# Reordering the attention of layer 2 in a vision-transformer tower on one Trainium2 core: four key products, exponentials and turned probabilities in another order, one filler product

## The chip, the cores and the metric

The kernel runs on one core of a Trainium2 chip. The metric is the device time of one execution in microseconds; where several executions were timed, their median. A profile is one execution, taken by the hardware profiler; its times count from the first instruction. Five engines run their own instruction streams and wait for each other on semaphores: TensorE (PE, with its weight loads as PEld), VectorE (DVE), ScalarE (ACT), GpSimd (POOL) and SyncE (SP).

## The reference

32 images of 84x84 are cut into 5x5 patches, so N = 25 tokens each, T = 800 tokens, C = 192 channels. A patch embedding and four post-norm layers follow. The part of this case is the third of the four, called layer 2 in the kernel, with 12 heads of 16 channels and two sets of queries and keys:

```python
def _L1_attn_ref(x, Wq, Wk, Wv, lambda_p, Wo, bo):
    q = (x @ Wq).reshape(B, N, 2, H, D).transpose(2, 0, 3, 1, 4)
    k = (x @ Wk).reshape(B, N, 2, H, D).transpose(2, 0, 3, 1, 4)
    v = (x @ Wv).reshape(B, N, H, D).transpose(0, 2, 1, 3)
    out1 = _attn(q[0], k[0], v)
    out2 = _attn(q[1], k[1], v)
    out = out1 - jnp.exp(lambda_p) * out2
    return out.transpose(0, 2, 1, 3).reshape(B, N, C) @ Wo + bo
...
h = _layernorm(h + _L1_attn_ref(h, ...), axis=-1)
```

Before it stand a linear attention (layer 0) and a mixture of 8 experts, 2 per token (layer 1); behind it an attention whose queries, keys and values come through adapters (layer 3), which the kernel computes with the same helpers as its "call 1".

## The kernel before

The program is written engine by engine, and the order on each engine is the order of the text; nothing is scheduled by a tool. The stage of this case runs from about 170 to 220 us.

The images form G = 8 groups of 4 images (100 tokens). Queries and keys come from split products (`split_job`, L1035 to L1041: five products of 400 columns each) for two halves of the tokens, 400 each; the first half serves groups 0 to 3, the second groups 4 to 7. ScalarE copies a query stack to `qT` (`queries_done`, L1191) or a key stack to `k_bd` (`keys_done`, L1360). A key stack is written four times, each copy multiplied by the mask of one head of four (`HQ` = 4), so that one product makes the scores of four heads. For the second half the stack of job 0 goes another way: ScalarE copies it once to `hwT`, and GpSimd makes the masked copies (L651).

A group g passes through these steps, each on one engine:

- PE, `scores(g)` (L962): 24 products in two or more banks of PSUM. For g >= 2 it waits until VectorE has read the group two before.
- DVE, `shift(g)`: the maximum (L1836) and the difference to `s1` (L1837).
- ACT, `exp_out(g)` (L1368): exponentials to `e1`, which has two buffers (g % 2). In layer 2 it waits for `p1_ready` of group g - 2, since GpSimd reads that buffer in `add_sets`.
- DVE, `norm(g)`: sum (L1846), reciprocal (L1847), factor with lambda (L1850, 24 columns), and the scaled exponentials in place (L1851, 600 columns).
- POOL, `add_sets(g)` (L640, L641): the two sets added to `p1`.
- PE, `turn(g)` (L972): the probabilities turned into bank 4.
- ACT, `p1T_out(g)` (L1191): the copy of bank 4 to `p1T`.
- PE, `times_v(g)` (L985): 12 products with the block-diagonal values `v_bd` into bank 5. It waits for `p1T_out(g)` and for `o_out(g - 1)`.
- ACT, `o_out(g)` (two copies, L1191): bank 5 to `oa` and `ob`.
- PE, `project(t)` (L996, L997) of a tile of 128 tokens, once its groups are there.

GpSimd also places the values in `v_bd` (`place_values`, L631) between these steps. VectorE's order is written out: shift 0, shift 1, norm 0, shift 2, norm 1, shift 3, norm 2, norm 3, shift 4, shift 5, norm 4, shift 6, norm 5, shift 7, norm 6, norm 7. `keep_busy` (L684) issues products whose result nobody reads; it stands at several places where PE waits. Scores 4 wait for `qk_act` 10, which is ScalarE's last query copy of the second half (`split_out(1, 5)`), and for `qk_pool`, GpSimd's masked keys.

Of the kernel before, what the change touches and what calls it, by code (L numbers as in the profile page):

```python
# [20 lines left out]
ALU = mybir.AluOpType  # L21
# [18 lines left out]
HALF = T // 2  # L40
# [20 lines left out]
HQ = 4  # L61
# [19 lines left out]
def rows(t):  # L81
    return min(128, T - 128 * t)


def view(ap, dims):

    return bass.AP(tensor=ap.tensor, offset=ap.offset, ap=[list(ap.ap[0])] + [list(d) for d in dims])


def build(nc, io):  # L90
    with ExitStack() as ctx:
        def sb(name, shape, dt=F32, scope=ctx):
            return scope.enter_context(nc.sbuf_tensor(name, shape, dt))

        def sem(name):
            return ctx.enter_context(nc.semaphore(name))

        ps = ctx.enter_context(nc.psum_tensor("ps", [128, 8, 512], F32))


        consts = sb("consts", [128, sum(w for _, w in CONSTS)])
        w0a, w0b = (sb(n, [r, sum(w for _, w in cols)]) for n, r, cols in (("w0a", 128, W0A), ("w0b", CB + 1, W0B)))
        w1a, w1b = (sb(n, [r, sum(w for _, w in cols)]) for n, r, cols in (("w1a", 128, W1A), ("w1b", 104, W1B)))

        def col(pack, cols, name, r0=0, r1=None):

            at = 0
            for n, width in cols:
                if n == name:
                    return pack[r0:r1 if r1 else pack.shape[0], at:at + width]  # L110
                at += width
            raise KeyError(name)

        ident = col(consts, CONSTS, "ident")
        head_mask1 = col(consts, CONSTS, "mask1")
# [59 lines left out]
        hwT = sb("hwT", [128, 32 * B], scope=late)  # L175
# [59 lines left out]
        k_bd = sb("k_bd", [128, 3, HQ, T])  # L235
# [67 lines left out]
        qk_ready, qk_act, qk_dve, qk_pool = sem("qk_ready"), sem("qk_act"), sem("qk_dve"), sem("qk_pool")  # L303
        s1_ready, s1_shifted, s1_exp = sem("s1_ready"), sem("s1_shifted"), sem("s1_exp")
# [190 lines left out]
        def _(pool):  # L495
# [138 lines left out]
            def add_sets(g):  # L634

                pool.wait_ge(e_scaled, g + 1)
                if g >= 2:
                    pool.wait_ge(p1T_ready, g - 1)
                blk = e1[:, g % 2, :, :].rearrange("p (a b c) m -> p a b c m", a=2, b=3)
                pool.tensor_tensor(p1[:, g % 2, 0:2, :, 0:N], blk[:, :, 0], blk[:, :, 1], ALU.add)  # L640
                pool.tensor_tensor(p1[:, g % 2, 2, :, 0:N], blk[:, 0, 2], blk[:, 1, 2], ALU.add).then_inc(p1_ready, 1)  # L641
# [5 lines left out]
            low_parts(1)  # L647
            add_sets(0)
            pool.wait_ge(qk_act, 5)
            for h in (0, 2):  # L650
                pool.tensor_tensor(k_bd[:, 0, h:h + 2, HALF:2 * HALF], view(hwT[:, 0:1], [[0, 2], [1, HALF]]),  # L651
                                   view(head_mask1[:, h:h + 1], [[1, 2], [0, HALF]]), ALU.mult).then_inc(qk_pool, 1)
            add_sets(1)
            pool.wait_ge(p1_ready, 2)
            place_values(0, 1, 0, 4)
# [17 lines left out]
        def last_group(t):  # L673

            return (128 * t + rows(t) - 1) // GT
# [3 lines left out]
        def _(pe):  # L679
# [274 lines left out]
            def scores(call, g, slots):  # L954
                if g >= 2:
                    pe.wait_ge(s1_shifted, G * call + g - 1)
                for bank, slot, row, stack in slots:
                    for i in range(IG):
                        tok = GT * g + N * i
                        keys = k_bd[row:row + 64, stack, :, tok:tok + N]  # L960
                        at = tok - HALF * (g // 4)
                        mm = pe.matmul(ps[32 * i:32 * i + 32, 2 * (g % 2) + bank, 4 * N * slot:4 * N * slot + 4 * N],  # L962
                                       qT[row:row + 64, stack, g // 4, at:at + 32], keys, start=True, stop=True)
                mm.then_inc(s1_ready, 1)

            def turn(call, g):
                n = G * call + g
                pe.wait_ge(p1_ready, n + 1)
                if g >= 1:
                    pe.wait_ge(p1T_done, n)  # L970
                for b in range(3):
                    mm = pe.transpose(ps[:, 4, 128 * b:128 * b + 128], p1[:, g % 2, b, :, :], ident[:, :])  # L972
                mm.then_inc(p1T_ready, 1)

            def times_v(call, g):
                n = G * call + g
                pe.wait_ge(p1T_done, n + 1)
                if g % 4 == 0:
                    pe.wait_ge(v_placed, 32 * call + 16 * (g // 4) + 16)
                if g >= 1:  # L980
                    pe.wait_ge(o1_done, n)
                for b, i in ((0, 0), (1, 0), (2, 0), (0, 1), (1, 1), (2, 1), (0, 2), (1, 2), (2, 2), (0, 3), (1, 3), (2, 3)):
                    rr = 64 * (b % 2)
                    at = (128 if b == 2 else 0) + N * i
                    mm = pe.matmul(ps[rr:rr + 64, 5, at:at + N], v_bd[:, IG * g + i, b, :],  # L985
                                   p1T[:, g % 2, b, 32 * i:32 * i + N], start=True, stop=True)
                mm.then_inc(o1_ready, 1)

            def project(call, t, wa, wb):
                pe.wait_ge(o1_done, G * call + last_group(t) + 1)  # L990
                if t >= 4 and t % 2 == 0:

                    pe.wait_ge(summed, PAIRS * (1 + call) + t // 2 - 1)
                cols = slice(128 * t, 128 * t + rows(t))
                out = ps[0:rows(t), PROJ_BANKS[t // 2], (t % 2) * C:(t % 2) * C + C]
                pe.matmul(out, oa[:, cols], wa, start=True, stop=False)  # L996
                pe.matmul(out, ob[:, cols], wb, start=False, stop=True).then_inc(proj_ready, 1)  # L997
# [73 lines left out]
            split_job(1, 5)  # L1071
            times_v(0, 0)
            turn(0, 1)
            pe.wait_ge(qk_act, 10)
            pe.wait_ge(qk_pool, 2)
            scores(0, 4, slots1)
            scores(0, 5, slots1)
            times_v(0, 1)
# [7 lines left out]
            turn(0, 4)  # L1086
            project(0, 1, wo1a, wo1b)
            times_v(0, 4)
            project(0, 2, wo1a, wo1b)
            turn(0, 5)  # L1090
            times_v(0, 5)
            turn(0, 6)
            project(0, 3, wo1a, wo1b)
# [95 lines left out]
        def _(act):  # L1189
            def copy(out, in_):  # L1190
                return act.activation(out, in_, ACT.Copy)  # L1191
# [161 lines left out]
            def queries_done(stack, n, src):  # L1353

                copy(qT[:, stack, n, 0:HALF], src).then_inc(qk_act, 1)

            def keys_done(m, stack, n, src):

                for h in range(HQ):
                    ins = act.activation(k_bd[0:m, stack, h, n * HALF:n * HALF + HALF], src, ACT.Copy, scale=head_mask1[0:m, h:h + 1])  # L1360
                ins.then_inc(qk_act, 1)

            def exp_out(call, g):
                act.wait_ge(s1_shifted, G * call + g + 1)
                if call == 0 and g >= 2:
                    act.wait_ge(p1_ready, g - 1)
                k = 12 if call else 24
                act.activation(e1[:, g % 2, 0:k], s1[:, g % 2, 0:k], ACT.Exp, scale=D1 ** -0.5).then_inc(s1_exp, 1)  # L1368

            def p1T_out(call, g):  # L1370
                act.wait_ge(p1T_ready, G * call + g + 1)
                if g >= 2 or call:
                    act.wait_ge(o1_ready, G * call + g - 1)
                copy(p1T[:, g % 2, :, :], ps[:, 4, 0:384]).then_inc(p1T_done, 1)

            def o_out(call, g):
                act.wait_ge(o1_ready, G * call + g + 1)
                copy(oa[:, GT * g:GT * g + GT], ps[:, 5, 0:GT])
                copy(ob[0:CB, GT * g:GT * g + GT], ps[0:CB, 5, 128:128 + GT]).then_inc(o1_done, 1)
# [13 lines left out]
            def split_out(n, job):  # L1393

                kind, stack = QK_ORDER[job]
                act.wait_ge(qk_ready, 6 * n + job + 1)
                src = ps[:, QK_BANKS[n][job], 0:HALF]
                if kind == "q":
                    queries_done(stack, n, src)
                else:  # L1400
                    keys_done(128, stack, n, src)
# [11 lines left out]
            split_out(1, 2)  # L1413
            p1T_out(0, 0)
            exp_out(0, 2)
            split_out(1, 3)
            exp_out(0, 3)
            split_out(1, 4)
            split_out(1, 5)
            p1T_out(0, 1)  # L1420
            o_out(0, 0)
            o_out(0, 1)
            exp_out(0, 4)
            p1T_out(0, 2)
            exp_out(0, 5)
            o_out(0, 2)
            p1T_out(0, 3)
            exp_out(0, 6)
            o_out(0, 3)
            p1T_out(0, 4)  # L1430
# [591 lines left out]
```

## Time and profile before

| | |
|---|---|
| median of 3 runs | 288.29 us |
| the three runs | 285.99, 288.29, 294.93 us |
| the profiled execution | 286.87 us |
| its span, first to last instruction | 285.1 us |
| PE, DVE, ACT, POOL busy | 258.6, 162.9, 121.3, 123.6 us |

The profiled execution's time is 1.8 us longer than its span: what lies before the first and behind the last instruction. A busy share is an average over stages, and idle time of an engine matters only where another waits for it. In a row of the timeline stand start, duration, engine, line, operation, output and inputs, shapes, and how many instructions the row merges; brackets at the end give the idle time before it and what ended it. A product of PE in 32-bit floats leaves two records, so x24 are 12 products of the program.

### The profile page before, as it was taken

The page shows a single profiled execution, that of the slowest core. Times are in us where ns is not written, and L with a number is a line of the kernel's source. Part 1 is how long each engine was busy: PE and PEld are TensorE (multiplying, and loading weights), DVE is VectorE, ACT ScalarE, POOL GpSimd, SP SyncE. Part 2 cuts the span into 40 slices and gives each one's busy share as a digit, 9 for nine tenths or more (in the row PEclk, how much of TensorE's full clock was granted, in tenths as well). Part 3 has the DMA queues.
Part 4 walks back from the last instruction along what each step waited for, and adds up shares of the span by engine and source line. Part 5 has one row for each costly group of instructions (what it writes and reads, how often), then busy time and mean ns, then how long its engine had stood idle before and what let it go on. Part 6 is the DMA issues. An engine that isn't in the chain of part 4 may idle for free.

```text
span 285.1 us, 6559 instructions
## 1 busy us (share of the span) xinstructions
PE 258.6 (91%) x2545; PEld 218.3 (77%) x2545; DVE 162.9 (57%) x486; ACT 121.3 (43%) x347; POOL 123.6 (43%) x191
## 2 busy tenths in 40 slices
PE   8989998976999999999999978998899799999990
PEld 8968678644999999999999538887777657667780
DVE  4676886885321332212330099899896474475874
ACT  5567868312442334433244005776441203763420
POOL 8762210316456655777432326857623100254311
PEclk9997999999999999999999999999689999999996
DMA  7999960161298999999200330000000000000002
GB/s 242 385 426 420 273 274 2 40 226 41 59 366 284 330 317 335 361 322 318 112 16 28 103 100 0 2 2 2 2 5 2 0 1 0 2 2 0 2 14 75
DMA packets 10113, 39.15 MB, mean 137 GB/s; under 512 B 1594, under 2 KB 5434, under 8 KB 7291
## 3 DMA queue, kind: packets, MB, share of 16 engines
q1 hardware_dynamic: 8163, 34.81, 33.9%
q0 software_dynamic: 1920, 3.93, 4.9%
q8 instruction: 20, 0.33, 0.4%
q14 instruction: 10, 0.08, 0.1%
HBM read 35.54 MB, written 3.19 MB: 136 GB/s over the span
## 4 chain that ended last, share of the span: by engine, by line
PE 66%; DVE 19%; ACT 4%; POOL 3%; issue 3%; DMA 3%; SPq 0%; POOLq 0%; ACTq 0%; DVEq 0%
PE ps L925 14%; PE ps L903 10%; PE ps L913 5%; PE ps L985 5%; PE ps L951 4%; PE ps L1121 3%; PE ps L972 2%; PE ps L996 2%; PE ps L962 2%; DVE s L1837 2%; PE ps L710 2%; DVE st L1836 2%; PE ps L810 2%; PE ps L997 1%; DVE st L1846 1%
## 5 line engine op out<-in xcount | busy, mean ns | idle before, releaser
L631 POOL COPY v_bd<-v_f 32x192 f32<-32x192 f32 x64 | 23.0, 359 | 34.3 <-ACT v_f L1191 30.4
L1321 ACT ACTIVATE hid<-ps,w1t 128x128 f32<-128x128 f32 x72 | 19.9, 376 | 34.7 <-PE ps L914 31.1
L577 POOL DMA_INDIRECT y_rows<-ys,to_row x20 | 19.8, 990 | 25.6 <-DVE ys L1793 23.2
L571 POOL DMA_INDIRECT xs<-x_rows,from_row x20 | 19.7, 983 | 22.0 <-PE ps L891 10.5
L1775 DVE COPY xga<-ps 128x128 f32<-128x128 f32 x20 | 5.8, 291 | 40.2 <-PE ps L891 39.9
L547 POOL TENSOR_TENSOR rstd<-veps,neg_half 128x2 f32<-128x2 f32 (+1 forms) x16 | 10.6, 664 | 41.6 <-DVE veps L1645 41.5
L925 PE MATMUL ps<-w1t,hid 128*128 128x192 f32 x144 | 24.6, 326 | 0.0
L684 PE MATMUL ps<-w1a,consts 128*128 128x384 f32 x66 | 22.7, 492 | 1.3 <-DVE h_tok L1627 1.3
L925 PEld LDWEIGHTS ps<-w1t,hid 128*128 128x128 f32 x144 | 23.3, 190 | 0.0
L985 PEld LDWEIGHTS ps<-p1T,v_bd 128*64 128x64 f32 x384 | 17.0, 142 | 5.3 <-issue 3.1
L985 PE MATMUL ps<-p1T,v_bd 128*64 128x25 f32 x384 | 18.6, 225 | 1.9 <-ACT p1T L1191 1.7
L684 PEld LDWEIGHTS ps<-w1a,consts 128*128 128x128 f32 x66 | 12.1, 190 | 9.8 <-DVE h_tok L1627 2.2
L903 PE MATMUL ps<-xga,w1t 128*128 128x128 f32 x144 | 18.7, 280 | 0.5 <-DVE xga L1775 0.5
L903 PEld LDWEIGHTS ps<-xga,w1t 128*128 128x128 f32 x144 | 17.2, 191 | 1.4 <-issue 0.7
L1836 DVE TENSOR_REDUCE st<-ps 128x24 f32<-128x600 f32 (+2 forms) x24 | 11.1, 462 | 12.2 <-PE ps L962 12.2
L1368 ACT ACTIVATE e<-s 128x600 f32<-128x600 f32 (+1 forms) x16 | 9.4, 586 | 14.2 <-DVE s L1837 14.2
L1360 ACT ACTIVATE k_bd<-ps,consts 128x400 f32<-128x400 f32 (+1 forms) x24 | 12.3, 600 | 0.8 <-PE ps L1041 0.8
L962 PE MATMUL ps<-k_bd,qT 64*32 64x100 f32 x576 | 11.4, 271 | 0.9 <-ACT qT L1191 0.9
L1837 DVE TENSOR_TENSOR s<-ps,st 128x600 f32<-128x600 f32 (+2 forms) x24 | 11.3, 470 | 0.8
L962 PEld LDWEIGHTS ps<-k_bd,qT 64*32 64x32 f32 x576 | 8.0, 113 | 4.8 <-issue 2.7
L1777 DVE COPY xgb<-ps 64x128 f32<-64x128 f32 x40 | 11.1, 278 | 0.6
L1793 DVE TENSOR_TENSOR ys<-ps,w1t 128x192 f32<-128x192 f32 x12 | 4.3, 357 | 12.4 <-PE ps L925 12.4
(301 smaller groups left out, 667.0 us busy)
## 6 DMA issues: line engine op xcount, KB each, us to landing
w1t<-in_wt SPq DMA_DIRECT2D x12, 1256.0 KB, 11.0
w1t_mid<-in_wt SPq DMA_DIRECT2D x3, 1256.0 KB, 11.4
w1t_top<-in_wt SPq DMA_DIRECT2D x3, 1256.0 KB, 10.9
pat<-in_pat SPq DMA_DIRECT2D x6, 496.0 KB, 5.8
w1t_low<-in_wt SPq DMA_DIRECT2D x2, 1256.0 KB, 7.5
w1a<-in_w1a SPq DMA_DIRECT2D x1, 1322.0 KB
y<-y_rows SPq DMA_DIRECT2D x6, 192.0 KB, 3.4
w1b<-in_w1b SPq DMA_DIRECT2D x1, 835.2 KB
```

The source lines that it names most:

```text
L571: pool.indirect_dma_start(xs[:, b, :], None, io["x_rows"], bass.IndirectOffsetOnAxis(from_row[:, j:j + 1], 0)).then_inc(gathered[b], 16)
L577: pool.indirect_dma_start(io["y_rows"], bass.IndirectOffsetOnAxis(to_row[:, j:j + 1], 0), ys[:, b, :], None).then_inc(scattered[b], 16)
L631: pool.tensor_copy(dst, src).then_inc(v_placed, 1)
L684: pe.matmul(ps[:, bank, 0:width], ident, w1a[:, 0:width] if width > 128 else ident, start=True, stop=True)
L903: mm = pe.matmul(hidden_out(j, k), w[:, 128 * k:128 * k + 128], xga[:, j % 2, :], start=(opens and k % HALF_HC == 0), stop=not opens, skip ...
L913: pe.matmul(hidden_out(j, k), w[0:CB, tail], xgb[0:CB, j % 2, :], start=(opens and k == 0), stop=not opens, skip_group_check=True)
L925: mm = pe.matmul(ps[:, Y_BANK[j % 2], 0:C], hid[:, j % 2, 128 * k:128 * k + 128], w[:, OUT_AT + C * k:OUT_AT + C * k + C], start=(k == 0), ...
L962: mm = pe.matmul(ps[32 * i:32 * i + 32, 2 * (g % 2) + bank, 4 * N * slot:4 * N * slot + 4 * N], qT[row:row + 64, stack, g // 4, at:at + 32 ...
L985: mm = pe.matmul(ps[rr:rr + 64, 5, at:at + N], v_bd[:, IG * g + i, b, :], p1T[:, g % 2, b, 32 * i:32 * i + N], start=True, stop=True)
L1321: ins = act.activation(hid[:, j % 2, 128 * k:128 * k + 128], hidden_out(j, k), ACT.Relu, bias=weights(j)[:, B1_AT + k:B1_AT + k + 1])
L1836: link(dve.tensor_reduce(top2, src, AX.X, ALU.max))
L1837: ins = dve.tensor_tensor(s, src, over(top2, N), ALU.subtract)
```

## The change

Five edits, all in the attention of layer 2. No arithmetic changes, except that one product more is computed and not read.

1. GpSimd masks the key stack in four products of 400 columns, one per head, where it used two of 800 columns; PE waits for four.
2. PE gets one 384-column filler product into bank 2 ahead of scores 4, behind a wait for VectorE's shift of group 3.
3. PE turns group 5 ahead of projection 2.
4. ScalarE does the exponentials of group 3 ahead of the key copies of job 3 (`split_out(1, 3)`), where they stood behind them.
5. ScalarE copies the turned probabilities of group 2 ahead of the exponentials of group 4, and those of group 3 ahead of `o_out` of group 2.

```diff
@@ GpSimd
             pool.wait_ge(qk_act, 5)
-            for h in (0, 2):
-                pool.tensor_tensor(k_bd[:, 0, h:h + 2, HALF:2 * HALF], view(hwT[:, 0:1], [[0, 2], [1, HALF]]),
-                                   view(head_mask1[:, h:h + 1], [[1, 2], [0, HALF]]), ALU.mult).then_inc(qk_pool, 1)
+            for h in range(HQ):
+                pool.tensor_tensor(k_bd[:, 0, h, HALF:2 * HALF], hwT[:, 0:HALF],
+                                   view(head_mask1[:, h:h + 1], [[0, HALF]]), ALU.mult).then_inc(qk_pool, 1)
             add_sets(1)
@@ PE
             turn(0, 1)
+            pe.wait_ge(s1_shifted, 4)
+            keep_busy(2, 1, 384)
             pe.wait_ge(qk_act, 10)
-            pe.wait_ge(qk_pool, 2)
+            pe.wait_ge(qk_pool, HQ)
             scores(0, 4, slots1)
...
             times_v(0, 4)
+            turn(0, 5)
             project(0, 2, wo1a, wo1b)
-            turn(0, 5)
             times_v(0, 5)
@@ ScalarE
             exp_out(0, 2)
+            exp_out(0, 3)
             split_out(1, 3)
-            exp_out(0, 3)
             split_out(1, 4)
             split_out(1, 5)
             p1T_out(0, 1)
             o_out(0, 0)
             o_out(0, 1)
+            p1T_out(0, 2)
             exp_out(0, 4)
-            p1T_out(0, 2)
             exp_out(0, 5)
+            p1T_out(0, 3)
             o_out(0, 2)
-            p1T_out(0, 3)
             exp_out(0, 6)
```

ScalarE between the exponentials of group 2 and the copy p1T of group 1, before (`e1` is an exponential, `k_bd` a masked key copy, `qT` a query copy):

```order
L1368 ACTIVATE e1<-s1 128x600
L1360 ACTIVATE k_bd<-ps,consts 128x400 x4
L1368 ACTIVATE e1<-s1 128x600
L1191 ACTIVATE qT<-ps 128x400 x2
L1191 ACTIVATE p1T<-ps 128x384
```

and after (its lines are numbered two higher from here on):

```order
L1370 ACTIVATE e1<-s1 128x600 x2
L1362 ACTIVATE k_bd<-ps,consts 128x400 x4
L1193 ACTIVATE qT<-ps 128x400 x2
L1193 ACTIVATE p1T<-ps 128x384
```

One exponential has moved ahead of four key copies; what follows is the same.

ScalarE behind that, from the two `o_out` of groups 0 and 1, before (`p1T` is the copy of the turned probabilities, `oa` and `ob` are one `o_out`):

```order
L1191 ACTIVATE oa<-ps 128x100
L1191 ACTIVATE ob<-ps 64x100
L1368 ACTIVATE e1<-s1 128x600
L1191 ACTIVATE p1T<-ps 128x384
L1368 ACTIVATE e1<-s1 128x600
L1191 ACTIVATE oa<-ps 128x100
L1191 ACTIVATE ob<-ps 64x100
L1191 ACTIVATE p1T<-ps 128x384
L1368 ACTIVATE e1<-s1 128x600
```

and after:

```order
L1193 ACTIVATE oa<-ps 128x100
L1193 ACTIVATE ob<-ps 64x100
L1193 ACTIVATE p1T<-ps 128x384
L1370 ACTIVATE e1<-s1 128x600 x2
L1193 ACTIVATE p1T<-ps 128x384
L1193 ACTIVATE oa<-ps 128x100
L1193 ACTIVATE ob<-ps 64x100
```

The copy of group 2 now stands ahead of the exponentials of groups 4 and 5, that of group 3 behind both.

PE at scores 4 and at projection 2, as one difference (L684 is the filler, L962 scores 4 and 5, L972 a turn, L985 products with the values, L996 and L997 a projection):

```order
 L985 MATMUL ps<-p1T,v_bd 64x25 x12
 L972 MATMUL ps<-consts,p1 128x128 x3
+L684 MATMUL ps<-w1a,consts 128x384
 L962 MATMUL ps<-k_bd,qT 32x100 x48
 L985 MATMUL ps<-p1T,v_bd 64x25 x12
...
-L996 MATMUL ps<-w1a,oa 128x192
-L997 MATMUL ps<-w1b,ob 128x192
-L972 MATMUL ps<-consts,p1 128x128 x3
+L972 MATMUL ps<-consts,p1 128x128 x3
+L996 MATMUL ps<-w1a,oa 128x192
+L997 MATMUL ps<-w1b,ob 128x192
 L985 MATMUL ps<-p1T,v_bd 64x25 x12
```

The filler has come between the turn of group 1 and scores 4, and the turn of group 5 has moved ahead of a projection.

## Rows read from the trace of the kernel before

**Rows 1.** Page: busy time, share of the span and instructions of each engine.

```profile
PE 258.6 (91%) x2545; PEld 218.3 (77%) x2545; DVE 162.9 (57%) x486; ACT 121.3 (43%) x347; POOL 123.6 (43%) x191
```

**Rows 2.** Chain of waits, 188 to 203 us: start us, us, what.

```profile
187.68 0.70 DVE st L1836
...
195.12 0.11 DVE st L1850
...
200.42 0.48 ACT p1T L1191
200.91 0.04 issue
200.95 1.21 PE ps L985 x24
```

**Rows 3.** Timeline of DVE, 188 to 206 us.

```profile
190.24 1.50 DVE L1850 TENSOR_TENSOR st<-st,lam 128x24 f32<-128x24 f32 x1
191.77 0.78 DVE L1851 TENSOR_TENSOR e<-e,st 128x600 f32<-128x600 f32 x1
...
195.12 0.18 DVE L1850 TENSOR_TENSOR st<-st,lam 128x24 f32<-128x24 f32 x1
...
198.20 0.77 DVE L1836 TENSOR_REDUCE st<-ps 128x24 f32<-128x600 f32 x1
...
201.20 0.77 DVE L1846 TENSOR_REDUCE st<-e 128x24 f32<-128x600 f32 x1
...
204.28 0.78 DVE L1836 TENSOR_REDUCE st<-ps 128x24 f32<-128x600 f32 x1 [0.91 <-PE ps L962]
```

**Rows 4.** Timeline of POOL, 181 to 213 us.

```profile
183.32 0.96 POOL L617 TENSOR_TENSOR x_lo<-xpa,x_hi 128x400 fp32r<-128x400 f32 x1 [0.27 <-POOL v_bd L631]
...
188.69 3.01 POOL L651 TENSOR_TENSOR k_bd<-hwT,consts 128x800 f32<-128x800 f32 x2
192.64 0.62 POOL L640 TENSOR_TENSOR p<-e 128x200 f32<-128x200 f32 x1 [0.94 <-DVE e L1851]
193.21 0.41 POOL L641 TENSOR_TENSOR p<-e 128x100 f32<-128x100 f32 x1
...
212.15 0.40 POOL L641 TENSOR_TENSOR p<-e 128x100 f32<-128x100 f32 x1
```

**Rows 5.** Timeline of ACT, 189 to 203 us.

```profile
192.46 2.08 ACT L1360 ACTIVATE k_bd<-ps,consts 128x400 f32<-128x400 f32 x4
194.36 0.76 ACT L1368 ACTIVATE e<-s 128x600 f32<-128x600 f32 x1
194.96 0.96 ACT L1191 ACTIVATE qT<-ps 128x400 f32<-128x400 f32 x2
...
199.81 0.70 ACT L1368 ACTIVATE e<-s 128x600 f32<-128x600 f32 x1 [0.98 <-DVE s L1837]
200.42 0.47 ACT L1191 ACTIVATE p1T<-ps 128x384 f32<-128x384 f32 x1
```

**Rows 6.** Timelines of PE, 164 to 172, 189 to 206 and 204 to 220 us.

```profile
165.27 3.49 PE L684 MATMUL ps<-w1a,consts 128*128 128x384 f32 x10 [1.26 <-DVE h_tok L1627]
...
195.97 1.40 PE L962 MATMUL ps<-k_bd,qT 64*32 64x100 f32 x96 [0.92 <-ACT qT L1191]
197.30 1.11 PE L985 MATMUL ps<-p1T,v_bd 128*64 128x25 f32 x24
198.34 0.55 PE L972 MATMUL ps<-consts,p 128*128 128x128 f32 x3
...
200.95 1.21 PE L985 MATMUL ps<-p1T,v_bd 128*64 128x25 f32 x24 [1.15 <-ACT p1T L1191]
202.92 1.25 PE L962 MATMUL ps<-k_bd,qT 64*32 64x100 f32 x48
204.11 1.90 PE L985 MATMUL ps<-p1T,v_bd 128*64 128x25 f32 x24
...
212.89 0.55 PE L972 MATMUL ps<-consts,p 128*128 128x128 f32 x3
...
216.72 1.11 PE L985 MATMUL ps<-p1T,v_bd 128*64 128x25 f32 x24
```

**Rows 7.** Windows: us, busy us of each engine, granted clock, DMA share, GB/s.

```profile
198.30:201.70 3.40, 2.25 (x30) 1.69 (x29) 3.33 (x5) 1.85 (x5) 2.95 (x9) 1.00 0.00 0
201.70:208.50 6.80, 6.80 (x138) 5.79 (x136) 5.65 (x11) 2.62 (x8) 3.49 (x8) 0.51 0.01 2
```

## The prediction

> **What bounds the kernel now.** I read the page first, then the windows by stage, then the chain of waits, then the timeline of each engine where the chain runs. On the page PE is 91% busy and no other engine is over 57% [rows 1], which says little, because the diff touches 30 us of 285: the attention of layer 2, from 188 to 220 us. There the chain of waits leaves PE. From 187.7 to 195.2 us it runs on DVE alone, then over POOL and ACT's copy of the turned probabilities, and returns to PE at 200.95 [rows 2]. So DVE sets the pace from 188 to about 203: every one of its instructions starts as the last ends [rows 3]. PE only waits at two places: 0.92 us before scores 4 and 5, for ACT's last query copy, and 1.15 us before the products with the values of group 2, for ACT's copy p1T [rows 6]. After that the granted clock is half (0.51, the 1.2 GHz level) from 201.7 to 208.5 us [rows 7], and PE is full: products with the values take 1.90 us there and 1.11 elsewhere [rows 6]. From 212.9 PE runs almost without a gap to the end of the stage. What the change is worth is therefore read from three things: when scores 4 starts, when p1T of group 2 is copied, and whether the clock is halved.
>
> **The four products on POOL.** Before, two products of 128x800 take 1.53 us each and 3.01 together [rows 4]. While they run, DVE's tiny product L1850 (0.18 us at 195.12) takes 1.50 and ends when POOL's second product ends [rows 3, 4]. So the change's idea is right: DVE loses 1.3 us there. The price of a 128x400 product is not in the trace; its bounds are half of 1.53 (0.76) and 0.96, which another POOL product of 128x400 takes. The sums of 200 and 100 columns (0.62 and 0.41) leave 0.20 fixed per instruction, so I take (1.53 - 0.20) / 2 + 0.20 = 0.86, with starts 0.81 apart. Then POOL's second piece ends at 188.69 + 0.81 + 0.86 = 190.36; L1850, waiting since 190.24, gets in and ends 190.54; the third piece runs to 191.40; DVE's L1851 (0.78) to 192.18; the fourth piece to 193.04. DVE is 0.37 us ahead (192.18 against 192.55), not 1.3, since L1851 collides in its turn.
>
> What happens to POOL matters more. It still owes the sums of group 1 (L640, L641: 0.98 together [rows 4]), and they end at 193.04 - 0.05 + 0.96 = 193.95, against 193.62. They cannot come earlier: in either kernel POOL's 3.0 us of products, DVE's 0.18 and 0.78 and POOL's 0.98 follow each other from 188.69, which makes at least 193.6. With pieces of 0.96 they end at 194.4.
>
> Here the row and a rule are weighed. The row shows DVE kept out until POOL's second product ended; the two products started 1.5 us apart with L1850 arriving just after the second had begun, so it doesn't show whether DVE would be let in between two queued products. The Trainium skill (SBUF — State Buffer, section "SBUF: two separate sides") says that the pair of ports which the two engines share is an exclusive lock held for the whole instruction, and that whoever starts first gets it. By that rule DVE gets in after the second piece, as above. If POOL kept it through its queue, L1850 would wait to 188.69 + 3 x 0.81 + 0.86 = 191.98, DVE would be 0.3 us later than now and POOL's sums would still end near 193.9. The forecast stands with either.
>
> **Exponentials of group 3 ahead of the keys (ACT).** The exponential of group 3 overwrites the buffer that the sums of group 1 read, so it waits for them. Today it stands behind four key copies (192.46 to 194.4) and starts at 194.36 without a wait, 0.7 us after the sums [rows 5]. Moved ahead, it is due at 192.46 and waits to 193.95 + 0.04 = 193.99. ACT stands still for 1.5 us with four key copies and two query copies queued behind, for which PE waits at scores 4. The start of the keys moves from 192.46 to 193.99 + 0.60 = 194.59; the keys still take 1.90 from start to start and the two queries 0.95, so the last query is done at 197.44 instead of 195.92. Scores 4 start at 197.48, 1.5 us later (bounds: 1.2 with the sums at 193.62, 1.95 with them at 194.4).
>
> Who pays? DVE wants scores 4 at 198.20 today [rows 3]. They take 0.73 and are there at 198.21, so DVE starts them at 198.25: the whole delay lands in DVE's slack, and DVE's lead of 0.37 is lost. The path isn't longer yet, but all margin is gone.
>
> **The filler at scores 4.** It waits for DVE's group 3 (past by 194), and one 384-column product is two records, 0.35 apart (ten in 3.49 us [rows 6]): 0.65 us. It stands from 194.85 to 195.5, when PE has nothing until 197.48. Its cost is nothing, hidden by that wait; without the wait it would cost 0.65. It leaves PE idle 1.95 us in one piece, where before it was 0.92.
>
> **p1T of group 2 ahead of the exponentials of group 4.** Today ACT does the exponentials at 199.81 and then p1T at 200.42, though group 2 was turned at 198.9 [rows 5, 6]. With scores 4 and 5 late, PE does the value products of group 1 at 198.81 (was 197.30) and turns group 2 at 199.85 (was 198.34). ACT copies p1T at 200.44, so nothing is gained at that place: value products of group 2 start at 201.2 (200.95). And the exponentials of group 4, now behind o_out and p1T, start at 200.81 (199.81), so DVE's sum L1846 of group 4 starts at 201.55 (201.20): 0.35 later. Then the order pays: PE need not wait again, turns group 3 and has scores 6 started at 202.6 at full clock or 203.5 at half (202.92 in the trace). DVE, which waited 0.91 us for scores 6 until 204.28 [rows 3], begins them between 203.8 and 205.0. The other swap, p1T of group 3 before o_out of group 2, moves two short copies by 0.4 us and I put it at 0.
>
> **Turn 5 ahead of projection 2.** Turn 5 comes 0.76 us earlier, and projection 2 covers the copy p1T. But turn 6 starts at 212.89, and its sums are ready at 212.55 [rows 4, 6]: at most 0.33 us, less where DVE is late. I take 0.
>
> **The sum.** I stepped all four engines through the new orders to the start of the last value products of the stage, with the durations above and in the rows. The same stepping of the old order starts them at 217.2 where the trace has 216.72 [rows 6], so I use differences. With the clock halved from 201.7 to 208.5 as before: 0.4 us earlier. With full clock throughout: 1.6 earlier. With the same 6.8 us at half clock beginning at 198.3: 1.2 later. Behind this stage nothing changes, so these carry to the end. The profiled execution took 286.87 us (span 285.1 and 1.8 around it); the runs shown have a median of 288.29, and all four times one of 287.6. My forecast is the first case: 287.6 - 0.4 = 287.2. No change that can be told: about 2% (5.8 us) is what a measurement of this kernel can tell from none.
>
> **Rivals.** A: the clock stays full. For it: the 1.15 us gap at 200 goes, and the clock fell just behind it [rows 7]; the filler adds work. Against: a longer gap stands at 195.5. It gives 287.6 - 1.6 = 286.0. B, the slower side: the gap of 1.95 us before scores 4 halves the clock at about 198, when PE is late already and the value products of groups 1 and 2, the turns and scores 6 are all on the path. For it: today the clock fell behind a shorter gap; against: today's 0.92 us gap there did nothing. It decides where the half clock begins before about 200; price +1.2, 288.8, and up to 1.6 with long pieces. C: the pieces don't let DVE in between; DVE is 0.3 us later from 192, scores 4 then cost DVE nothing, and the sum is -0.1: 287.5. That would mean that the split doesn't do what it is for.
>
> **Chances.** Forecast 0.42, A 0.25, B 0.25, C 0.08. A and B lie within 2%. The range takes both, 286.0 to 289.2, and 1.2 to 1.6 us on each side for how far the shown runs lie apart (286.0 to 288.3 with one at 294.9): 284.8 to 290.8. Faster by over 2% would need more than both gaps (2.1 us) and what half clock costs there (3.4 us) hold together: 0.02. Slower by over 2% only by such an outlying execution: 0.03.
>
> **What would show it.** Right: ACT idle about 1.5 us before the exponentials of group 3; scores 4 near 197.5; DVE's L1850 near 0.3 us and L1851 at 0.8 or stretched; POOL's sums of group 1 no earlier than 193.6; the exponentials of group 4 near 200.8. Wrong: scores 4 at or before 196, or POOL's sums before 193.5, or the stage's end moved by more than 2 us with the clock as before.

## The result, and the profile after

The changed kernel is slower: 290.69 us median (289.63 to 290.94, 4 runs) against 287.14 of the kernel before, ratio 1.013 with a 95% interval of 1.0101 to 1.0159. The forecast was 287.2 in a range of 284.8 to 290.8, "no change that can be told". The median lies inside the range by 0.1 us, which is luck: the ratio is clear of 1 on the side of rival B, and not for B's reason. Ratios here leave out disturbed executions, in which a lower clock was granted and the time is some per cent longer (294.93 us among the runs of before); medians take all.

The profiled execution took 290.69 us, its span is 288.9 (before 285.1). None of the 3.8 us comes from what lies ahead of the scores: the changed kernel starts the scores of group 0 at 181.34, 0.3 us earlier (181.63). Four engines of the stage follow, first POOL and DVE where the key products run. The rows are from the changed kernel's timelines; L1852 is L1850 of before, L1853 is L1851 (answer to [rows 3, 4]):

```profile
188.41 3.83 POOL L651 TENSOR_TENSOR k_bd<-hwT,consts 128x400 f32<-128x400 f32 x4
192.20 0.61 POOL L640 TENSOR_TENSOR p<-e 128x200 f32<-128x200 f32 x1
192.78 0.40 POOL L641 TENSOR_TENSOR p<-e 128x100 f32<-128x100 f32 x1
```

```profile
189.96 0.18 DVE L1852 TENSOR_TENSOR st<-st,lam 128x24 f32<-128x24 f32 x1
190.18 1.35 DVE L1853 TENSOR_TENSOR e<-e,st 128x600 f32<-128x600 f32 x1
...
202.96 0.77 DVE L1838 TENSOR_REDUCE st<-ps 128x24 f32<-128x600 f32 x1
...
206.52 0.78 DVE L1838 TENSOR_REDUCE st<-ps 128x24 f32<-128x600 f32 x1
```

The tiny product no longer stands still (0.18, was 1.50), the large one now does (1.35, was 0.78). DVE gains 0.7 us at this place, counted from scores 0. DVE takes scores 6 at 202.96 without a wait, where it waited until 204.28.

ACT (answer to [rows 5]):

```profile
191.56 0.73 ACT L1370 ACTIVATE e<-s 128x600 f32<-128x600 f32 x1
193.26 0.70 ACT L1370 ACTIVATE e<-s 128x600 f32<-128x600 f32 x1 [0.97 <-POOL p L641]
193.88 2.03 ACT L1362 ACTIVATE k_bd<-ps,consts 128x400 f32<-128x400 f32 x4
195.78 0.91 ACT L1193 ACTIVATE qT<-ps 128x400 f32<-128x400 f32 x2
```

The exponentials of group 3 wait 0.97 us for POOL's sums of group 1, and ACT's key and query copies behind them are late by about that.

PE from scores 4 to the end of the stage (answer to [rows 6]):

```profile
194.59 0.81 PE L684 MATMUL ps<-w1a,consts 128*128 128x384 f32 x2
196.74 1.41 PE L962 MATMUL ps<-k_bd,qT 64*32 64x100 f32 x96 [1.34 <-ACT qT L1193]
198.08 1.11 PE L985 MATMUL ps<-p1T,v_bd 128*64 128x25 f32 x24
...
202.04 0.85 PE L962 MATMUL ps<-k_bd,qT 64*32 64x100 f32 x48
...
205.99 1.11 PE L985 MATMUL ps<-p1T,v_bd 128*64 128x25 f32 x24
207.69 0.55 PE L972 MATMUL ps<-consts,p 128*128 128x128 f32 x3 [0.60 <-POOL p L641]
...
209.55 1.11 PE L985 MATMUL ps<-p1T,v_bd 128*64 128x25 f32 x24 [0.65 <-ACT p1T L1193]
211.26 0.55 PE L972 MATMUL ps<-consts,p 128*128 128x128 f32 x3 [0.60 <-POOL p L641]
...
213.03 1.91 PE L985 MATMUL ps<-p1T,v_bd 128*64 128x25 f32 x24
214.86 0.90 PE L972 MATMUL ps<-consts,p 128*128 128x128 f32 x3
...
216.99 1.91 PE L985 MATMUL ps<-p1T,v_bd 128*64 128x25 f32 x24
```

Until 206 PE is ahead of the kernel before: scores 6 start at 202.04 (202.92), the value products of group 4 at 205.99 (208.97). Then it has caught up with DVE and waits three times, 0.60, 0.65 and 0.60 us. From 211.7 its products take 1.7 times as long. The windows say why (answer to [rows 7]; the columns are those of [rows 7], and the last three are granted clock, DMA share and GB/s):

```profile
198.30:201.70 3.40, 3.40 (x56) 2.87 (x53) 3.22 (x6) 2.16 (x5) 2.97 (x9) 1.00 0.00 0
...
208.30:211.70 3.40, 2.15 (x32) 1.75 (x31) 3.19 (x8) 1.58 (x6) 0.96 (x2) 1.00 0.01 2
211.70:218.50 6.80, 6.80 (x58) 5.83 (x58) 4.10 (x15) 1.36 (x4) 2.35 (x4) 0.50 0.00 0
218.50:225.30 6.80, 6.33 (x25) 4.78 (x25) 3.89 (x15) 0.39 (x2) 1.24 (x2) 0.50 0.01 2
```

The half clock (1.2 GHz level) has moved. In the kernel before it lay from 201.7 to 208.5, where DVE sets the pace and PE has time to spare. Now it lies from 211.7 to 225.3, twice as long, where PE is the bound. Timelines are best compared from a common start. In the table all numbers but those of the last column are microseconds from the first product of scores 0, each a difference of two times in one trace; "end" is the end of the span:

| kernel | scores 4 | scores 6 | values 7 | layer 3 turns | end | half clock, length at time from span start |
|---|---|---|---|---|---|---|
| before | 14.3 | 21.3 | 35.1 | 38.8 | 103.5 | 6.8 at 201.8 |
| changed | 15.4 | 20.7 | 35.7 | 42.0 | 107.6 | 13.7 at 211.7 |

"Values 7" are the last value products of the stage, "layer 3 turns" the first turns of normalised tokens behind it. At values 7 the changed kernel is 0.6 us behind, from there to the turns it loses 2.6 more, and another 0.9 until the first products behind them with the clock back (227.10, before 223.31). From there to the end nothing is lost.

### The profile page after: what moved, and what is told of

It reads as the page before. It is cut to its first block, busy times and chain, and to the rows that moved or that the text cites. A ratio compares the mean times of both kernels' runs of the same rounds, so it can differ in the third digit from the quotient of the medians.

```text
span 288.9 us, 6565 instructions
## 1 busy us (share of the span) xinstructions
PE 263.3 (91%) x2547; PEld 221.4 (77%) x2547; DVE 162.7 (56%) x486; ACT 120.8 (42%) x347; POOL 124.2 (43%) x193
## 4 chain that ended last, share of the span: by engine, by line
PE 65%; DVE 17%; ACT 5%; POOL 5%; issue 4%; DMA 3%; SPq 0%; POOLq 0%; ACTq 0%; DVEq 0%
PE ps L925 14%; PE ps L903 10%; PE ps L913 5%; PE ps L985 4%; PE ps L951 4%; PE ps L1123 3%; PE ps L996 2%; PE ps L972 2%; PE ps L710 2%; PE ps L810 2%; PE ps L962 2%; PE ps L997 1%; DVE s L1839 1%; DVE stats L1640 1%; PE ps L794 1%
## 5 line engine op out<-in xcount | busy, mean ns | idle before, releaser
L571 POOL DMA_INDIRECT xs<-x_rows,from_row x20 | 19.6, 981 | 22.1 <-PE ps L891 11.0
L684 PE MATMUL ps<-w1a,consts 128*128 128x384 f32 x68 | 25.1, 519 | 1.3 <-DVE h_tok L1629 1.3
L985 PEld LDWEIGHTS ps<-p1T,v_bd 128*64 128x64 f32 x384 | 17.7, 147 | 4.8 <-issue 3.2
L684 PEld LDWEIGHTS ps<-w1a,consts 128*128 128x128 f32 x68 | 13.0, 198 | 10.3 <-DVE h_tok L1629 2.2
L985 PE MATMUL ps<-p1T,v_bd 128*64 128x25 f32 x384 | 19.3, 229 | 1.0 <-ACT p1T L1193 0.7
L1370 ACT ACTIVATE e<-s 128x600 f32<-128x600 f32 (+1 forms) x16 | 9.3, 582 | 14.3 <-DVE s L1839 13.3
L1193 ACT ACTIVATE xpa<-ps 128x500 f32<-128x500 f32 (+3 forms) x6 | 1.8, 356 | 25.1 <-PE ps L701 25.1
L962 PE MATMUL ps<-k_bd,qT 64*32 64x100 f32 x576 | 10.6, 252 | 1.3 <-ACT qT L1193 1.3
L962 PEld LDWEIGHTS ps<-k_bd,qT 64*32 64x32 f32 x576 | 7.5, 105 | 5.4 <-issue 2.6
```

What stands on the lines that cost most here:

```text
L571: pool.indirect_dma_start(xs[:, b, :], None, io["x_rows"], bass.IndirectOffsetOnAxis(from_row[:, j:j + 1], 0)).then_inc(gathered[b], 16)
L684: pe.matmul(ps[:, bank, 0:width], ident, w1a[:, 0:width] if width > 128 else ident, start=True, stop=True)
```

## The experiments

Three theories were set against each other. Clock: the reordering takes away the gap behind which the clock fell at 201.7, PE then catches up with DVE and gets its gaps later, and the clock falls where PE is the bound. Wait: the 0.97 us that ACT waits ahead of the exponentials of group 3 passes down the stage. Chance: where the clock falls is luck of the execution. Each run states its ratio to the kernel before, measured beside it.

**e3, three more fillers.** In the changed kernel:

```diff
+            pe.wait_ge(s1_shifted, 7)
+            keep_busy(0, 1, 384)
             turn(0, 5)
             project(0, 2, wo1a, wo1b)
+            keep_busy(0, 1, 384)
             times_v(0, 5)
+            keep_busy(0, 1, 384)
             turn(0, 6)
```

> The changed kernel with three more fillers of 384 columns (0.65 us each) on PE, where it now waits 0.60, 0.65 and 0.60 us: ahead of turn 5, ahead of the value products of group 5 and ahead of turn 6. Clock theory (the loss is the 13.65 us of half clock from 211.7 to 225.3, which begins because PE has gaps from 206 on): the clock stays at its higher level through the stage, the last value products start near 214 to 215.5 and the kernel takes 285 to 287 us. Wait theory (the loss is ACT's wait ahead of the exponentials of group 3 and what it delays): half clock or not, the time stays at 290 to 291. Chance theory (where the clock falls is luck of the runs): one or two of the runs fast, the others slow.

Measured: 285.35 us, ratio 0.9937 (0.9894 to 0.998). From scores 0 to 280 us the clock stays full. More work on PE made the kernel 5.3 us faster than the changed one and 0.6% faster than the one before. The wait theory falls: ACT's wait is still there (scores 4 at 15.4 from scores 0, as in the changed kernel). Chance falls too as the reason for the difference between these two kernels: 283.69 to 286.83 in 7 runs against 289.63 to 290.94 in 4.

**e1, turn 5 back behind projection 2.**

```diff
-            turn(0, 5)
             project(0, 2, wo1a, wo1b)
+            turn(0, 5)
```

> The changed kernel with turn 5 behind projection 2 again. Clock theory: PE's gaps ahead of turn 5 and of the value products of group 5 are joined or shifted (projection 2 fills the wait for turn 5's sums), so PE is as idle in total; the fall at 211.7 should stay and the time with it, 290 to 291, unless this swap alone made the gaps, then 286 to 288. Wait theory: no more than 0.5 us change from 290.7.

Measured: 289.98 us, ratio 1.0095 (1.0064 to 1.0125). The two gaps of 0.60 and 0.65 become one of 1.27, and the clock falls at 210.8 for 13.7 us, inside the gap of 0.60 ahead of turn 6. The swap isn't the cause, and no gain or loss by it can be told here.

**e2, exponentials of group 3 back.**

```diff
-            exp_out(0, 3)
             split_out(1, 3)
+            exp_out(0, 3)
```

> The changed kernel with the exponentials of group 3 behind the key copies again, so that ACT doesn't wait for POOL's sums of group 1 and scores 4 start 1.0 us earlier. Wait theory: 287 to 288. Clock theory: DVE's pace from 198 on is the same, so PE still has its gaps from 206 on; the half clock stays in the tail and the time is 289.5 to 291.

Measured: 290.53 us, ratio 1.0115 (1.004 to 1.019). Scores 4 start at 14.3, 1.1 us earlier than in the changed kernel, scores 6 and values 7 too (19.6, 34.9), and the end is still at 107.1, since the clock falls at 211.6 for 13.7 us. That is the clock theory's forecast; the wait theory's was 287 to 288.

**e4, only the p1T copies moved.** Of the five edits this one alone, in the kernel before:

```diff
+            p1T_out(0, 2)
             exp_out(0, 4)
-            p1T_out(0, 2)
             exp_out(0, 5)
+            p1T_out(0, 3)
             o_out(0, 2)
-            p1T_out(0, 3)
             exp_out(0, 6)
```

> The kernel before with only the copies of turned probabilities moved (group 2 ahead of the exponentials of group 4, group 3 ahead of o_out of group 2). Clock theory: the 1.15 us gap at 200 goes, the half clock moves from 201.7 to later, into the part where PE is the bound; 288.5 to 291 us. Wait theory: copies earlier, nothing later, 285.5 to 287.5, faster than before.

Measured: 290.78 us, ratio 1.0136 (1.0112 to 1.0159): the whole loss. In its trace the value products of group 2 have no gap ahead of them, PE waits five times behind them (0.71, 0.41, 0.24, 1.06 and 0.60 us), and the half clock lies from 212.4, 13.7 us long. The first two of these waits:

```profile
203.22 1.08 PE L985 MATMUL ps<-p1T,v_bd 128*64 128x25 f32 x24 [0.71 <-ACT ob L1191]
...
205.49 0.55 PE L972 MATMUL ps<-consts,p 128*128 128x128 f32 x3 [0.41 <-POOL p L641]
```

**e5, no reordering, only fillers in the gap.** This one takes the copies out of the question: nothing is moved, PE gets dummy work while it waits at 200 us.

```diff
             project(0, 0, wo1a, wo1b)
+            keep_busy(7, 1, 384)
+            keep_busy(7, 1, 256)
             times_v(0, 2)
```

> The kernel before with no reordering at all, only two fillers (384 and 256 columns, 1.08 us) in the 1.15 us gap ahead of the value products of group 2, where PE waits anyway. Clock theory: the half clock at 201.7 doesn't come, PE runs ahead of DVE as in the changed kernel, gets its gaps after 206, and the clock falls near 212 for the tail instead: 289.5 to 291.5 us, though no instruction was moved and no wait added. Rival (the loss belongs to ACT's new order of copies): 286 to 288, as before.

Measured: 290.67 us, ratio 1.0154 (1.0107 to 1.02). Two fillers in idle time cost 1.5%, though the value products of group 2 start no later (19.3 us from scores 0 in both). The timeline of its PE:

```profile
199.37 1.24 PE L684 MATMUL ps<-w1a,consts 128*128 128x384 f32 x4
200.69 1.11 PE L985 MATMUL ps<-p1T,v_bd 128*64 128x25 f32 x24
...
202.98 1.11 PE L985 MATMUL ps<-p1T,v_bd 128*64 128x25 f32 x24
...
209.70 1.11 PE L985 MATMUL ps<-p1T,v_bd 128*64 128x25 f32 x24 [1.13 <-ACT p1T L1193]
211.41 0.72 PE L972 MATMUL ps<-consts,p 128*128 128x128 f32 x3 [0.60 <-POOL p L641]
211.92 0.85 PE L996 MATMUL ps<-w1a,oa 128*128 128x192 f32 x2
```

The value products of group 3 take 1.11 us at 202.98, where before they took 1.90 at 204.11 [rows 6]: the clock didn't fall at 201.7. Then gaps of 0.24, 1.13 and 0.60 us follow, and the projection at 211.92 is at half clock. The loss so needs nothing of ACT's new order but that the gap at 200 is closed.

**e6, one of the three late fillers.** The changed kernel with the filler ahead of turn 6 alone:

```diff
             times_v(0, 5)
+            pe.wait_ge(s1_shifted, 7)
+            keep_busy(0, 1, 384)
             turn(0, 6)
```

> The changed kernel with one filler of 384 columns ahead of turn 6 only, of the three that made 285.35. Clock theory: it fills 0.6 of 1.85 us of gaps just before the clock falls at 211.7; if the fall hangs on how much PE did just before, 285 to 287.5; if one isn't enough, 289.5 to 291. Wait theory: 290.7 either way.

Measured: 284.31 us (10 runs, 283.27 to 286.0), ratio 0.9938 (0.9909 to 0.9967), a little below what was expected. Timeline of its PE:

```profile
208.65 0.55 PE L972 MATMUL ps<-consts,p 128*128 128x128 f32 x3 [0.60 <-POOL p L641]
...
210.50 1.11 PE L985 MATMUL ps<-p1T,v_bd 128*64 128x25 f32 x24 [0.65 <-ACT p1T L1195]
211.55 0.91 PE L684 MATMUL ps<-w1a,consts 128*128 128x384 f32 x2
212.30 0.49 PE L972 MATMUL ps<-consts,p 128*128 128x128 f32 x3
...
215.81 1.11 PE L985 MATMUL ps<-p1T,v_bd 128*64 128x25 f32 x24
```

The gaps of 0.60 and 0.65 us are still there, only the third is filled, and that is enough: the last value products take 1.11 us (1.91 in the changed kernel). One filler, 0.75 us from its start to that of the turn behind it (211.55 to 212.30), in a gap that was there anyway, is worth about 6 us: 6.4 between the medians, 5.7 between the traces from scores 0, 5.5 by the two ratios.

**e7, p1T copies and late fillers only.** The four other edits left out; fillers where this order has its gaps:

```diff
+            pe.wait_ge(s1_shifted, 7)
             turn(0, 5)
+            keep_busy(0, 2, 384)
             times_v(0, 5)
+            keep_busy(0, 1, 384)
             turn(0, 6)
```

> The kernel before with the p1T copies moved (alone 290.8) and three late fillers: two of 384 columns ahead of the value products of group 5, one ahead of turn 6. The four products, the exponentials of group 3, turn 5 and the filler at scores 4 are as before. Clock theory: full clock through the stage, 285 to 286.5, so that the four other edits are worth under 0.5 us. If they matter: 286.5 to 288.

Measured: 285.25 us, ratio 0.9952 (0.9922 to 0.9982), as expected in the median. In its profiled execution, behind gaps of 0.73 us ahead of the value products of group 3 and 0.41 ahead of turn 4, the clock fell at 203.8 for 6.8 us. There PE has time to spare, and values 7 start at 36.6, layer 3's turns at 40.4.

```profile
201.33 1.08 PE L985 MATMUL ps<-p1T,v_bd 128*64 128x25 f32 x24 [0.73 <-ACT ob L1194]
...
203.61 0.74 PE L972 MATMUL ps<-consts,p 128*128 128x128 f32 x3 [0.41 <-POOL p L641]
```

Up to this turn the instructions of e7 and e4 are the same, and so are the gaps within 0.02 us; in e4's trace the clock held there. So with the p1T copies moved, chance does decide whether it falls at this place. How often can't be read from one trace of each.

**e8, three late fillers, exponentials of group 3 back.** e3 with the edit of e2.

> The changed kernel with the three late fillers and the exponentials of group 3 behind the key copies again. With the clock full, the stage goes at DVE's pace: scores 4 come 1.0 us earlier but DVE takes them 0.3 us earlier at best; 284.9 to 285.5, against 285.35. Wait theory: 1 us better than with them ahead, 284.3.

Measured: 284.06 us (9 runs), ratio 0.994 (0.9909 to 0.9971). The time is below the expected 284.9 and close to the wait theory's 284.3, but the two ratios (0.994, and e3's 0.9937) do not differ, and the traces are 0.2 us apart from scores 0 to the end (101.7, 101.9). Values 7 start 0.2 us earlier than in e3 (33.3, 33.5), though scores 4 start 1.1 us earlier. At full clock DVE's pace absorbs all but 0.2 of the wait.

**e9, control.** The filler ahead of turn 6 in the kernel before:

```diff
             times_v(0, 5)
+            pe.wait_ge(s1_shifted, 7)
+            keep_busy(0, 1, 384)
             turn(0, 6)
```

> Control: the kernel before with one filler of 384 columns ahead of turn 6, the one that brought the changed kernel from 290.7 to 284.3. Clock theory: here the clock falls at 201.7 already and is back before the filler, and PE doesn't wait at turn 6, so the filler only costs: 287 to 288, no faster than before. Rival (the filler at turn 6 helps any kernel): 284 to 285.5.

Measured: ratio 1.0004 (0.9958 to 1.0051); its two fastest runs took 286.14 and 286.25 us (expected 287 to 288), two others 296.02 and 299.41. The half clock lies at 200.7 for 6.8 us as before, and the filler brings nothing here, where the clock doesn't fall behind that place without it either.

**e10, no filler at scores 4.** The change's own filler taken out:

```diff
-            pe.wait_ge(s1_shifted, 4)
-            keep_busy(2, 1, 384)
             pe.wait_ge(qk_act, 10)
```

> The changed kernel without its filler at scores 4, so that PE stands still for 2.0 us in one piece there. Rival B of the prediction (a long wait at scores 4 halves the clock at about 198): the clock falls near 198 and the time differs from 290.7, 288 to 289.5 by the prediction's price. Clock theory as it stands now (what counts is how little PE does in all, in the stretch before the fall near 212): if PE keeps the clock across that one gap, 290 to 291 with the fall near 212.

Measured: 288.87 us in the profiled execution and 295.68 to 297.94 in the three others, so there is no ratio, and only the one trace can be read. PE:

```profile
197.07 1.54 PE L962 MATMUL ps<-k_bd,qT 64*32 64x100 f32 x96 [2.00 <-ACT qT L1191]
198.54 1.90 PE L985 MATMUL ps<-p1T,v_bd 128*64 128x25 f32 x24
```

and its windows:

```profile
194.80:198.20 3.40, 1.40 (x97) 1.17 (x97) 3.21 (x6) 2.84 (x8) 2.45 (x6) 1.00 0.00 0
198.30:201.70 3.40, 3.40 (x42) 3.07 (x30) 2.69 (x4) 0.77 (x4) 2.95 (x9) 0.50 0.02 5
```

Behind a gap of 2.00 us in one piece the clock falls at 198.2 for 13.7 us. That is rival B's mechanism. In the changed kernel, which differs by the filler alone, 1.34 us of gap are left and the clock doesn't fall there. With one trace of each this makes the filler the likely reason, no more: chance is not ruled out at this place. Scores 6 start at 23.5 instead of 20.7, values 7 at 37.0 instead of 35.7; then the full clock is back for the tail, and the end is at 105.4, ahead of the changed kernel's 107.6. My own expectation, with the fall near 212, was wrong.

**e11, the one filler, exponentials of group 3 back.** e6 with the edit of e2.

> The changed kernel with the exponentials of group 3 behind the keys again and the one filler ahead of turn 6: 283.8 to 284.5, at full clock through the stage; the best kernel so far by 0 to 0.5 us. Wait theory: 1.0 us faster than with the exponentials ahead, 283.3.

Measured: 284.95 us (6 runs), ratio 0.9965 (0.9926 to 1.0005). Its trace is the shortest of all from scores 0 on (101.5; e6 101.9, e8 101.7), its time no better than e6's. The order of the exponentials is worth at most 0.4 us in a trace and can't be told in the times (expected were 283.8 to 284.5).

**e12, two products on POOL, one filler.** e6 with the four products undone:

```diff
-            for h in range(HQ):
-                pool.tensor_tensor(k_bd[:, 0, h, HALF:2 * HALF], hwT[:, 0:HALF],
+            for h in (0, 2):
+                pool.tensor_tensor(k_bd[:, 0, h:h + 2, HALF:2 * HALF], view(hwT[:, 0:1], [[0, 2], [1, HALF]]),
...
-            pe.wait_ge(qk_pool, HQ)
+            pe.wait_ge(qk_pool, 2)
```

> The changed kernel with the one filler ahead of turn 6, and POOL's key stack masked in two products again. If the split is worth what DVE's L1850 stood still for less what L1851 does now (0.6 us in the changed kernel's trace, DVE's group 3 earlier by 0.7): 284.6 to 285.2, against 284.3. If it is worth nothing: 284.0 to 284.5.

Measured: 286.78 us (4 runs), ratio 1.0021 (0.9976 to 1.0066); expected were 284.6 to 285.2 if the split is worth something. DVE, ACT and PE in its trace:

```profile
189.16 1.49 DVE L1854 TENSOR_TENSOR st<-st,lam 128x24 f32<-128x24 f32 x1
190.68 0.78 DVE L1855 TENSOR_TENSOR e<-e,st 128x600 f32<-128x600 f32 x1
```

```profile
193.01 0.70 ACT L1372 ACTIVATE e<-s 128x600 f32<-128x600 f32 x1 [1.51 <-DVE s L1841]
```

```profile
196.50 1.41 PE L962 MATMUL ps<-k_bd,qT 64*32 64x100 f32 x96 [1.89 <-ACT qT L1195]
```

The stall of 1.49 us is back, and ACT waits 1.51 us instead of 0.97. It now waits for DVE's shift of group 3 (done at 192.98), which the stall made late, and no longer for POOL's sums (done at 192.54). Scores 4 start at 16.0 (15.4) and the stage ends 0.85 us later than in e6 (values 7 at 34.4 against 33.5). So the split is worth about 0.9 us in the trace when the exponentials stand ahead; the 2.5 us between the two medians are more than that. The record holds a hint at the rest: e12's four runs took 285.09 (the profiled one), 286.10, 287.46 and 288.06 us at mean granted clocks of 0.993, 0.987, 0.978 and 0.962, where e6's ten have 0.982 to 0.994. The longer runs had more half clock; where it lay can't be read, since they have no trace. PE's gap at scores 4 is 1.89 us here, with the filler ahead of it, and in the trace the clock holds.

The traces side by side (same anchor and columns as above):

| kernel | scores 4 | scores 6 | values 7 | layer 3 turns | end | half clock, length at time from span start |
|---|---|---|---|---|---|---|
| e4 only p1T | 14.3 | 19.6 | 35.7 | 42.1 | 107.6 | 13.7 at 212.4 |
| e5 fillers at 200 | 14.3 | 20.9 | 35.9 | 42.3 | 107.7 | 13.7 at 211.7 |
| e2 exp 3 back | 14.3 | 19.6 | 34.9 | 41.3 | 107.1 | 13.7 at 211.6 |
| e10 no filler at scores 4 | 15.4 | 23.5 | 37.0 | 40.8 | 105.4 | 13.7 at 198.2 |
| e12 two products | 16.0 | 21.3 | 34.4 | 38.1 | 102.8 | none in the stage |
| e6 one filler | 15.4 | 20.7 | 33.5 | 37.3 | 101.9 | none in the stage |
| e11 exp 3 back, one filler | 14.3 | 19.6 | 33.1 | 36.9 | 101.5 | none in the stage |

## Why the prediction was wrong

**The step that failed is the sum's clock.** The prediction stepped the engines through the new order and then laid the half clock of before over it: 6.8 us long, at 201.7 (forecast), at 198.3 (rival B), or nowhere (rival A). In the changed kernel it is 13.7 us long and begins at 211.7. None of the three cases had it there, and there it costs most, since PE has no time to spare from 212 on. The stepping itself was good: at full clock it put the last value products 1.6 us before those of the kernel before, and e6, the changed kernel with one filler more and at full clock, has them 1.6 us before (33.5 against 35.1). What the prediction left out is where PE would wait in the new order behind 206: it names no gap there, and the trace has 0.60, 0.65 and 0.60 us, for POOL's sums at turns 5 and 6 and for ACT's copy between them. Rival A's argument, "the 1.15 us gap at 200 goes, and the clock fell just behind it", should have been followed by the question where PE's slack goes. DVE sets the pace from 188 to about 211, so in these kernels the slack didn't go away: in the kernel before, the gap at 200 and the 6.8 us of half clock took it up, and with both gone it came back as gaps behind 206. e5 shows that without any reordering.

**Rival B** was right about its mechanism and wrong about the kernel. Behind a gap of 2 us at scores 4 the clock did fall (e10, at 198.2). In the changed kernel it didn't: the filler, which I costed at nothing and gave no worth, stands there, and the gap that is left is 1.34 us, forecast 1.95. The length of that gap alone doesn't decide, since e12's trace bears 1.89. I had B at a price of 1.2 us at values 7 for 6.8 us of half clock; e10 has 1.9 for 13.7.

**The exponentials of group 3.** ACT's wait was forecast at 1.5 us and is 0.97; scores 4 start 1.1 us later, forecast 1.5. The mechanism held, the term was mis-sized in one place: I let L1850 wait for POOL's second piece and pay its full 0.18 afterwards, while L1852 ran in 0.18 us as if nothing were there, so POOL's four pieces took 3.83 us instead of 4.35. That the sums of group 1 can't come earlier than before held only to 0.2 us: measured from scores 0 they ended at 11.8 against 12.0. In absolute time that is 193.18, and "POOL's sums before 193.5" was one of the prediction's signs of being wrong. The prediction also named only one of two things that these exponentials need. The other is DVE's shift of group 3; in the kernel before it ends at 194.06, behind the sums (193.62), and in the changed kernel at 193.03, just ahead of them (193.18). Without the split it would have been the later one, as e12 shows. That DVE absorbs the wait held too: e11 against e6 gives 0.4 us at values 7 for 1.1 us at scores 4.

**The four products.** 0.85 us for each of the first three (forecast 0.86), starts 0.81 apart, and 1.39 for the fourth. DVE was let in between two queued pieces, so rival C falls: L1853 took 0.57 us longer and then held up POOL's fourth piece, which makes the 3.83. The Trainium skill (SBUF — State Buffer, "SBUF: two separate sides") has the shared ports as an exclusive lock for the whole instruction. Both traces agree, but for 0.1 us: the one that comes second takes longer by what is left of the other's instruction, less 0.13 or 0.14 us. L1850 grew by 1.32 us with 1.46 of POOL's product left, L1853 by 0.57 with 0.70 left, and POOL's fourth piece by 0.54 with 0.68 of L1853 left. L1852 came with 0.11 left and didn't grow at all. The sum's 0.4 us of lead for DVE became 0.7, and DVE takes scores 4 at 197.63, 0.3 us earlier than before counted from scores 0, where the forecast had its lead lost.

**The other edits.** Turn 5: forecast 0, shown 0 (e1: values 7 0.35 us later at half clock, the time 0.7 us less; neither can be told from none). p1T of group 2: forecast nothing gained at that place, and that was about right (the value products of group 2 start 19.2 us after scores 0, before 19.3; in e4, where scores 4 are not late, they start at 18.1). The gain is behind them: PE has no wait and runs at full clock, and scores 6 start 0.6 us earlier. That is how PE caught up with DVE.

**The chances.** I gave 0.95 to "within 2%", which held, but the interval of 1.0 to 1.6% is well apart from no change, and with a spread of 1.3 us among the four runs of the changed kernel this was measurable. The prediction's 2% for what a measurement can tell from none was too coarse.

What stays open: why the half clock lasts 13.7 us in some traces and 6.8 in others, why the clock fell at 203.8 in the one execution of e7 and not in that of e4 behind the same gaps, why e12's trace bears a gap of 1.89 us at scores 4 and e10's doesn't bear 2.00, and where the half clock lay in e12's longer runs.

## What to carry to other kernels

Where another engine sets the pace, closing a gap of PE can open others later (e5: 1.15 us closed, 0.24, 1.13 and 0.60 opened). Before closing one, step the new order through and see where PE waits next, and whether PE is the bound in what follows. The filler was worth about 6 us in the last gap ahead of a stretch where PE is the bound, and nothing in the kernel before, whose clock had fallen and come back earlier (e6, e9). A filler or an earlier copy at another gap cost 1.5% and 1.4% (e5, e4). Compare traces from a common start inside the program, and put the granted clock beside every stage of it before believing that a reordering was good or bad.

## What the runs showed of the hardware that was not expected

Several short gaps can cost the clock. It fell behind three gaps of 0.60 to 0.65 us with products between them (PE busy 2.15 of 3.40 us between 208.3 and 211.7), and not with the last of the three filled (e6); e2 falls and e11, the same kernel with that gap filled, doesn't. One gap of 0.58 us ahead of the value products of group 5 (at 211.84) did nothing in the kernel before. The clock fell behind 2.00 us in one piece (e10), and not behind 1.34 or 1.89 with a filler ahead (the changed kernel, e12). Counted from scores 0 the late fall came at 30.3 to 30.4 us in four kernels (changed, e2, e4, e5) and at 29.6 in e1. The changed kernel's four runs have mean granted clocks of 0.955 to 0.968 and e6's ten 0.982 to 0.994, so the late fall is no accident of single executions; at 203.8 it is one (e7, e4). The Trainium skill (TensorE: Matmul & The Clock Gate, "A second HAM failure mode: psum-queue depth-cycling") tells of another kernel, with other products, in which short idles of TensorE between groups of products were frequent enough that the clock kept changing between its two levels. These runs agree that short idles can cost the clock, with gaps of 0.6 us.

Adding work made the program faster: 0.75 us of products that nobody reads, in a gap that was there anyway, took the changed kernel from 290.69 to 284.31 us.
